# Doubles joined inside the next up product, shared tiles at every second place, and four products moved between the second batch's turned rows

## The chip, the cores and the metric

The kernel runs on one core of a Trainium2 chip. The metric is the device time of one execution in microseconds (us). Three executions of the kernel before gave 403.53, 402.61 and 404.11 us. One further execution was recorded by the profiler, and all rows below come from it.

## What is computed

The reference is a block of two parts over x of shape (4, 512, 512); cut to what matters:

```python
# part 1, once for each of the 4 batches
sim = einsum(h @ Wq.T, h @ Wk.T) / scale           # 512 x 512
thr = the 153rd largest value of each row of sim
A   = sigmoid(sim) * (sim >= thr);  A = (A + A.T) / 2
x   = x + tanh(g_xattn) * ((1 - gamma) * layernorm(x) + gamma * A)
# part 2, over all 2048 rows of x2 = layernorm(x)
shared = (silu(x2 @ Wsg) * (x2 @ Wsu)) @ Wsd
top_val, top_idx = top_k(x2 @ router_w, 2)         # 8 experts
each row, weighted by sigmoid(top_val), goes through 2 of the 8 experts:
    (silu(gate) * up) @ down_w[e]
x = x + tanh(g_ffn) * (shared + sum of the row's 2 experts)
```

## The kernel before, in words

Every engine runs a list of calls that is written out by hand. Semaphores tie the lists together; nothing reorders them.

Part 1 goes batch by batch: `sim_tile` products, copied out by ScalarE (`sim_of`); a search for the threshold on VectorE (`count`, `move`, `last_count`, `best_below`, `threshold`) with help from ScalarE (`sign`); `mask_sim`; `turn_a` (transposes) and `add_turned`; layer norm (`normal`); `turn_x2`; `route` (router logits), `turn_logits`, `pick_experts`, and the tables that tell which row goes to which expert (`rank_pairs`, `one_hots`, `table`, `add_table`, `count_pairs`, `order_columns`, `name_rows`, `read_plan`). The tables are finished twice: `read_plan(0)` after two batches names the rows of the first 9 expert tiles, `read_plan(1)` after all four those of the other 25.

Part 2 is a list of 50 jobs `j`, each of 128 rows. 16 of them are shared-expert tiles ("S"), 34 are expert tiles ("M", tile `t`). From j = 23 on (t = 7) there are only expert tiles and j = t + 16. One expert tile passes through these steps:

- GpSimd: `gather(t)`, an indirect DMA of 128 rows into one of 4 slots
- VectorE: `weight_of(t)`, the row's weight
- TensorE: `turn_rows(t)` (4 transposes), `up(j)` (gate and up products), `turn_h(j)`, `down(j)`
- ScalarE: `turned_rows`, `silu_of(j)`, `turned_h(j)`, and `y_of(j)`, which writes the result to one of two buffers `y_sb[:, j % 2]`
- VectorE: `gate(j)`
- GpSimd: `scatter(t)`, an indirect DMA that adds 128 rows to the output

Scatters add to shared rows, so each waits for the one before it to land (`pool.wait_ge(scattered, 16 * t)`), and `y_of(j)` waits until the scatter of job j - 2 has landed. In a row of the trace a scatter is `out_dram<-y_sb,idx` (or `y_sb,tmp`) on L550, and a shared tile's plain store is on L512. TensorE's steps on neighbouring jobs interleave: `up(j+1)`, `turn_rows`, `down(j)`, `turn_h(j+1)`.

Nine of the expert tiles are mixed: their 128 rows are four units of 32 rows, each with an expert of its own (the word "shared tiles" in the title means these). A mixed tile's products run as groups 32 columns wide (L1288 and L1318) instead of 128 wide (L1292 and L1327). Its weights are first copied side by side: `stage_up` on VectorE (4 copies of 128x2048, L2014) and `stage_down` on ScalarE (4 copies of 128x1024, L783). Both stages have one buffer, so copies for the next mixed tile start only after the product of the last one. A mixed tile may hold a token twice ("doubles"). `fold(j)` on TensorE adds doubles up (one product on `y_sb`, L1244), and `folded_y(j)` on ScalarE copies the sum back (L787); only then may its scatter start. Before, the mixed tiles are t = 9, 12, 15, 18, 21, 24, 27, 30, 32.

A shared tile's `gate(j)` writes `hT[:, j % 2]` and waits for the `down` of job j - 2 (`dve.wait_ge(y_ps, j - 1)`), which reads the same half.

Of the kernel before, what the change touches and what calls it, by code (L numbers as in the profile page):

```python
# [16 lines left out]
P = 128  # L17
# [8 lines left out]
def flamingo_gated_block(nc, x, ctx_in, g_xattn, g_ffn, wq, wk, gamma_raw, router_w, gate_up_w, down_w,  # L26
# [38 lines left out]
    MIXED = (9, 12, 15, 18, 21, 24, 27, 30, 32)  # L65
# [14 lines left out]
    NJ = len(JOBS)  # L80

# [9 lines left out]
    def x_slot(j):  # L91
        kind, n = JOBS[j]
        return n % RT if kind == "S" else 2 + n % 2

# [16 lines left out]
    with ExitStack() as stack:  # L111
# [123 lines left out]
        etab_u = tmp[0:1, 3, 64:64 + UNITS].bitcast(I32)  # L235
        unit_gu = sim[:, :, :, :].rearrange("p b i n -> p b (i n)")
# [232 lines left out]
        def _(pool):  # L469
# [38 lines left out]
            def shared(j):  # L508
# [3 lines left out]
                G.dma_start(out_v[n // RT][:, n % RT], y_sb[:, j % 2], accum_op=ALU.add).then_inc(shared_out[j % 2], 16)  # L512
# [21 lines left out]
            def scatter(t):  # L534
# [7 lines left out]
                if t == 0:  # L542
                    for m in range(2):
                        pool.wait_ge(shared_out[m], 16 * RT)
                else:
                    pool.wait_ge(scattered, 16 * t)
                if t == EARLY:
                    for m in range(2):
# [3 lines left out]
                                     in_=y_sb[:, j % 2, :], in_offset=None, compute_op=ALU.add  # L552
# [101 lines left out]
        def _(act):  # L654
# [110 lines left out]
            def y_of(j):  # L765
                act.wait_ge(y_ps, j + 1)
                if j >= 2:
                    if is_m(j - 2):
                        act.wait_ge(scattered, 16 * m_count(j - 1))
                    else:  # L770
                        act.wait_ge(shared_out[j % 2], 16 * s_count_like(j))
                A.activation(y_sb[:, j % 2], y_b[j % 2][:, :], ACT.Copy, scale=gates[:, 1:2]).then_inc(y_done, 1)  # L772
# [12 lines left out]
            def folded_y(j):  # L785
                act.wait_ge(fold_ps, mixed_at(j) + 1)
                A.copy(y_sb[:, j % 2], f_b[0][:, :]).then_inc(folded, 1)  # L787
# [62 lines left out]
            sign(2, 0)  # L850
            y_of(1)
# [8 lines left out]
            sim_of(3, 2)  # L860
# [3 lines left out]
            sign(2, 1)  # L864
            sign(2, 2)
            probs(1)
            sim_of(3, 3)
            silu_of(4)
            silu_of(5)
            sign(2, 3)  # L870
            silu_of(6)
            affine(2)
            y_of(3)
            y_of(4)
            read_bad(2)
            turned_rows(0)
            silu_of(7)
            turned_rows(1)
# [68 lines left out]
            turned_rows(7)  # L947
            silu_of(21)
            y_of(19)
            silu_of(22)  # L950
            turned_rows(8)
            silu_of(23)
            y_of(20)
# [20 lines left out]
            stage_down(1, 1)  # L974
            silu_of(27)
            turned_rows(12)
            folded_y(25)
# [7 lines left out]
            turned_h(28)  # L985
            silu_of(29)
# [1351 lines left out]
```

## Time and profile before

| what | value |
|---|---|
| median of three runs | 403.53 us (402.61 to 404.11) |
| the profiled execution's own time | 402.77 us |
| its span, first to last instruction | 401.0 us |
| TensorE busy | 367.5 us, 92% of the span |
| VectorE, ScalarE, GpSimd busy | 228.9, 216.8, 134.1 us |
| granted TensorE clock, mean | 0.975 |

The span is what the rows of the trace describe; 1.8 us of the execution's own time lie around it. "PE" is TensorE, "PEld" its weight loads, "DVE" VectorE, "ACT" ScalarE, "POOL" GpSimd, "SP" the queue that issues plain DMAs. A row of a timeline gives start, duration, engine, line, operation and tiles, and in brackets how long the engine was idle before it and what ended the idle time. In the chain of work, durations are cut so that the pieces follow one another.

### The profile page before, as it was taken

Reading aid. Unit: us, or ns where it says so; the run is one execution under the profiler, and the core shown is the slowest. Engines: PE = TensorE matmul, PEld = TensorE weight load, DVE = VectorE, ACT = ScalarE, POOL = GpSimd, SP = SyncE. Lnnn points to the kernel's source line nnn. Section 1 sums busy time; section 2 is a strip of 40 time slices with the busy share of each in tenths; the row PEclk is TensorE's granted clock in tenths of the full one; section 3 lists DMA queues with packets and bytes.
Section 4 is the critical chain, followed back from the end, with each engine's and each line's share of the span. In section 5 each row is a group of like instructions: output and inputs, shape, how many; then the busy total and the mean of one; then the engine's idle time right before and its main releaser. Section 6 shows DMA issues by size and latency. Waiting matters only on the chain.

```text
span 401.0 us, 6566 instructions
## 1 busy us (share of the span) xinstructions
PE 367.5 (92%) x2018; PEld 202.8 (51%) x2021; DVE 228.9 (57%) x819; ACT 216.8 (54%) x422; POOL 134.1 (33%) x114
## 2 busy tenths in 40 slices
PE   8859889889999999999999999999999999998950
PEld 4314478467755688548955444444444444433310
DVE  1899999998998689852636652332415150505000
ACT  3594877484773696353121475455555647363620
POOL 2201121110534331322303363544536354544231
PEclk9977999999999999999999999999999999999995
DMA  7999971084676542467423444535354454544432
GB/s 215 384 386 382 391 249 13 15 242 130 188 133 184 161 76 32 52 147 172 50 33 79 80 63 97 83 77 107 54 106 66 93 86 78 103 65 96 52 45 33
DMA packets 29353, 51.12 MB, mean 127 GB/s; under 512 B 4614, under 2 KB 7942, under 8 KB 29318
## 3 DMA queue, kind: packets, MB, share of 16 engines
q0 software_dynamic: 9920, 22.16, 32.9%
q1 hardware_dynamic: 19110, 28.40, 20.2%
q8 instruction: 17, 0.28, 0.3%
q14 instruction: 18, 0.15, 0.1%
q10 hardware_dynamic: 288, 0.13, 0.1%
HBM read 28.60 MB, written 22.09 MB: 126 GB/s over the span
## 4 chain that ended last, share of the span: by engine, by line
PE 74%; DMA 9%; DVE 7%; ACT 4%; issue 3%; SPq 1%; POOLq 0%; POOL 0%; DVEq 0%; ACTq 0%
PE gate_up L1292 20%; PE down L1327 15%; PE gate_up L1281 14%; PE gate_up L1288 6%; DMA out_dram<-y_sb,idx 4%; PE turned_x L1263 4%; DMA out_dram<-y_sb,tmp 4%; PE down L1318 3%; PE turned_h L1302 2%; DMA xs<-in_x_dram 2%; PE down L1117 2%; DVE ge_words L1721 2%; PE front L1244 1%; PE front L1155 1%; ACT x L711 1%
## 5 line engine op out<-in xcount | busy, mean ns | idle before, releaser
L1292 PE MATMUL gate_up<-w_gu,xT 128*128 x200 | 89.9, 593 | 0.8 <-DVE hT L2036 0.7
L550 POOL DMA_INDIRECT out_dram<-y_sb,idx x25 | 49.6, 1985 | 73.9 <-DMA out_dram<-y_sb,tmp 26.6
L2031 DVE SCALAR_TENSOR_TENSOR h<-gate_up,p_t,silu 128x256 f32<-128x256 f32 x34 | 16.4, 482 | 80.9 <-ACT silu L745 72.0
L1281 PE MATMUL gate_up<-xT,w_shgu 128*128 128x128 f32 x512 | 59.9, 276 | 1.1 <-ACT xT L722 1.1
L1281 PEld LDWEIGHTS gate_up<-xT,w_shgu 128*128 128x128 f32 x512 | 58.6, 192 | 3.3 <-issue 2.0
L772 ACT ACTIVATE y_sb<-down,gates 128x512 f32<-128x512 f32 x50 | 34.2, 687 | 43.4 <-PE down L1327 28.4
L1292 PEld LDWEIGHTS gate_up<-w_gu,xT 128*128 128x128 f32 x200 | 36.3, 190 | 39.2 <-issue 39.1
L529 POOL DMA_INDIRECT xg<-x_rows,idx x34 | 40.2, 1182 | 36.4 <-DMA x_rows<-payl 15.5
L1327 PE MATMUL down<-w_dn,hT 128*128 x100 | 47.2, 596 | 0.0
L745 ACT ACTIVATE silu<-gate_up,p_t 128x256 f32<-128x256 f32 x34 | 16.1, 473 | 49.1 <-PE gate_up L1292 31.7
L2014 DVE COPY sim<-w_gu 128x2048 f32 x36 | 41.9, 1223 | 0.3 <-issue 0.2
L674 ACT ACTIVATE junk<-sim,probe 128x512 int8<-128x512 f32 x44 | 31.2, 713 | 13.3 <-DVE probe L1712 9.7
L783 ACT COPY xs<-w_dn 128x1024 f32 x36 | 36.0, 1045 | 0.5 <-issue 0.3
L1288 PE MATMUL gate_up<-sim,xT 128*32 128x512 f32 x288 | 32.8, 595 | 0.0
L763 ACT COPY xT<-turned_x 128x512 f32<-128x512 f32 x34 | 19.9, 585 | 20.0 <-PE turned_x L1263 19.3
L1327 PE MATMUL down<-w_shdn,hT 128*128 128x512 f32 x64 | 30.3, 599 | 0.0
L512 POOL DMA_DIRECT2D out_dram<-y_sb x16 | 15.7, 1025 | 42.4 <-ACT y_sb L772 42.3
L1263 PEld LDWEIGHTS turned_x<-ident,xg 128*128 128x128 f32 x136 | 16.0, 141 | 20.2 <-issue 19.9
L550 POOL DMA_INDIRECT out_dram<-y_sb,tmp x9 | 14.2, 1576 | 34.4 <-DVE p_junk L2021 26.3
L1327 PEld LDWEIGHTS down<-w_dn,hT 128*128 128x128 f32 x100 | 17.2, 190 | 13.3 <-issue 13.3
L2021 DVE SCALAR_TENSOR_TENSOR p_junk<-xg,oh_e 128x8 f32<-128x8 f32 x34 | 5.4, 161 | 30.1 <-DMA xg<-x_rows,idx 29.9
L1263 PE MATMUL turned_x<-ident,xg 128*128 128x128 f32 x136 | 21.0, 277 | 1.2 <-ACT xT L763 0.8
(222 smaller groups left out, 508.3 us busy)
## 6 DMA issues: line engine op xcount, KB each, us to landing
w_gu<-in_L_ffn_gate_up_w_dram SPq DMA_DIRECT2D x8, 1024.0 KB, 12.2
xs<-in_x_dram SPq DMA_DIRECT2D x4, 1024.0 KB, 6.4
w_dn<-in_L_ffn_down_w_dram SPq DMA_DIRECT2D x8, 512.0 KB, 10.7
out_dram<-xs SPq DMA_DIRECT2D x4, 1024.0 KB, 6.4
x_rows<-x SPq DMA_DIRECT2D x4, 1024.0 KB, 5.1
out_dram<-y_sb POOLq DMA_DIRECT2D x16, 256.0 KB, 4.4
w_gu<-in_ctx_dram SPq DMA_DIRECT2D x4, 256.0 KB, 5.3
xg<-x_rows,idx POOLq DMA_INDIRECT x34, 4.1
```

The lines of the kernel that those rows point to most:

```text
L529: G.indirect_dma_start(out=xg[:, t % XG, :], out_offset=None, in_=x2_rows[0:2 * N, :] if t < EARLY else x2_rows[:, :], in_offset=bass.Indi ...
L550: G.indirect_dma_start(out=out[0:2 * N, :] if t < EARLY else out[:, :], out_offset=bass.IndirectOffsetOnAxis(ap=rows, axis=0), in_=y_sb[:, ...
L674: ins = A.activation(junk[:, i - SHARE[b]], sim[:, b, i], ACT.Sign, scale=-1.0, bias=probe[:, k, i:i + 1], accum_out=sgn[:, k, i:i + 1])
L763: A.copy(xT[:, x_slot(j)], x_b[:, :].rearrange("p (c t) -> p c t", c=DC)).then_inc(xt_done, 1)
L772: A.activation(y_sb[:, j % 2], y_b[j % 2][:, :], ACT.Copy, scale=gates[:, 1:2]).then_inc(y_done, 1)
L783: A.copy(unit_dn[:, g], w_dn[:, bass.ds(e * (IC * D), IC * D)]).then_inc(dn_staged, 1)
L1263: mm = TE.transpose(x_b[:, c * P:(c + 1) * P], xg[:, t % XG, c * P:(c + 1) * P], ident[:, :])
L1281: mm = TE.matmul(g_b[j % 2][:, f * P:(f + 1) * P], w_shgu[:, c, f * P:(f + 1) * P], xT[:, x_slot(j), c], start=(c == 0), stop=(c == DC - 1))
L1288: mm = TE.matmul(g_b[j % 2][at, :], xT[:, x_slot(j), c, at], unit_gu[:, r, c * F2:(c + 1) * F2], start=(c == 0), stop=(c == DC - 1))
L1292: mm = TE.matmul(g_b[j % 2][:, :], xT[:, x_slot(j), c], w_gu[:, bass.ds(experts[n] * (DC * F2) + c * F2, F2)], start=(c == 0), stop=(c == ...
L1327: mm = TE.matmul(y_b[j % 2][:, :], hT[:, j % 2, c], w, start=(c == 0), stop=(c == IC - 1))
L2014: V.tensor_copy(unit_gu[:, g], w_gu[:, bass.ds(e * (DC * F2), DC * F2)]).then_inc(gu_staged, 1)
```

## The change

Four things are changed; the amount of arithmetic is not.

1. The mixed tiles move to t = 9, 11, 13, ..., 25. The last eight tiles (26 to 33) are then all ordinary ones. `stage_up`, `stage_down`, `folded_y` and `fold` move with them.
2. `fold(j)` is no longer a call of its own between `up` and `turn_rows`. It is issued in the middle of `up(j + 2)`, and `folded_y(j)` stands ahead of `silu_of(j + 2)`.
3. Around the second batch (`route(1)`, `turn_logits(1)`, `table(0)`) and in the plan of the later tiles (`order_columns(1)`, `order_units`, `name_rows(1)`) calls change places on TensorE, VectorE and ScalarE; `warm(4, 3)`, three products that compute nothing, is gone.
4. `CHAIN`, `Y_FROM`, `y_slot`, `y_user` and `y_at` are new names. `CHAIN` lists 0 to 33 in order and `Y_FROM` is 100 while jobs end at 49, so every wait and every address comes out as before.

```diff
-    MIXED = (9, 12, 15, 18, 21, 24, 27, 30, 32)
+    MIXED = (9, 11, 13, 15, 17, 19, 21, 23, 25)
...
-            def up(j):
+            def up(j, folds=None):
...
                     for c in range(DC):
+                        if c == DC // 2 and folds is not None:
+                            fold(folds)
...
             turn_a(1, 3)
+            pe.wait_ge(sim_ready, 14)
+            sim_tile(3, 2)
             down(1)
-            pe.wait_ge(sim_ready, 14)
+            pe.wait_ge(sim_ready, 15)
             rank_pairs(0)
             down(2)
+            pe.wait_ge(rank_used, 1)
+            sim_tile(3, 3)
...
-            pe.wait_ge(rank_used, 1)
-            sim_tile(3, 2)
+            down(3)
             route(1)
-            pe.wait_ge(y_done, 2)
-            warm(4, 3)
             turn_logits(1)
+            table(0)
             up(4)
...
             up(21)
             pe.wait_ge(logit_used, 4)
             count_pairs(1)
+            down(19)
+            order_columns(1)
             up(22)
-            order_columns(1)
             pe.wait_ge(rank_used, 4)
             table(3)
-            down(19)
             turn_rows(7)
+            down(20)
             order_units()
             turn_rows(8)
             up(23)
             name_rows(1)
-            down(20)
             up(24)
...
-            up(27)
-            fold(25)
+            up(27, 25)
             turn_rows(12)
...
             last_count(2)
-            gate(6)
+            gate(7)
             best_below(2)
             weight_of(0)
-            gate(7)
             threshold(2)
...
             place_units()
+            gate(22)
             read_plan(1)
-            gate(22)
...
             gate(31)
-            stage_up(3, 0)
-            stage_up(3, 1)
-            stage_up(3, 2)
-            stage_up(3, 3)
+            stage_up(4, 0)
+            stage_up(4, 1)
+            stage_up(4, 2)
+            stage_up(4, 3)
             weight_of(17)
```

What stands there in the order of instructions, at three places.

TensorE while the plan of the later tiles is made, before; `down1` is `down(19)`, `gate_up0` is `up(22)`, L1203 is `order_columns(1)`, L1194 `table(3)`, L1207 `order_units`, and the two L1263 are `turn_rows(7)` and `turn_rows(8)`:

```order
L1281 MATMUL gate_up0<-xT,w_shgu 128x128 x16
L1203 MATMUL front1<-el_b,upper 128x1
L1194 MATMUL front0<-tmp 128x128 x8
L1327 MATMUL down1<-w_shdn,hT 128x512 x2
L1254 TENSOR_LOAD etab
L1254 ISA x2
L1263 MATMUL turned_x<-ident,xg 128x128 x4
L1207 MATMUL front1<-el_b,upper 128x1
L1254 TENSOR_LOAD etab
L1254 ISA x2
L1263 MATMUL turned_x<-ident,xg 128x128 x4
```

The same place after the change:

```order
L1349 MATMUL down1<-w_shdn,hT 128x512 x2
L1221 MATMUL front1<-el_b,upper 128x1
L1299 MATMUL gate_up0<-xT,w_shgu 128x128 x16
L1212 MATMUL front0<-tmp 128x128 x8
L1272 TENSOR_LOAD etab
L1272 ISA x2
L1281 MATMUL turned_x<-ident,xg 128x128 x4
L1349 MATMUL down0<-w_shdn,hT 128x512 x2
L1225 MATMUL front1<-el_b,upper 128x1
L1272 TENSOR_LOAD etab
L1272 ISA x2
L1281 MATMUL turned_x<-ident,xg 128x128 x4
```

`down(19)` went ahead of `up(22)` and `order_columns(1)` with it; `down(20)` (`down0`), which stood behind `name_rows(1)`, now stands between the two turned rows.

TensorE at the first fold, before: the last half of the ordinary product `up(27)`, the fold (L1244), then `turn_rows(12)` and `down(26)`:

```order
L1292 ISA
L1292 MATMUL gate_up1<-w_gu,xT 128x512
L1292 ISA
L1292 MATMUL gate_up1<-w_gu,xT 128x512
L1244 MATMUL front0<-y_sb,x2 128x512
L1263 MATMUL turned_x<-ident,xg 128x128 x4
L1327 ISA
L1327 MATMUL down0<-w_dn,hT 128x512
L1327 ISA
L1327 MATMUL down0<-w_dn,hT 128x512
```

After the change, `down(25)`, `turn_h(26)`, and then `up(27)`, which is now a mixed tile:

```order
L1340 MATMUL down1<-xs,hT 32x512 x8
L1324 MATMUL turned_h<-ident,h 128x128 x2
L1308 MATMUL gate_up1<-sim,xT 32x512 x8
L1262 MATMUL front0<-y_sb,x2 128x512
L1308 MATMUL gate_up1<-sim,xT 32x512 x8
L1272 TENSOR_LOAD etab
L1272 ISA x2
L1281 MATMUL turned_x<-ident,xg 128x128 x4
```

The fold, 128 wide, now stands between the two halves of a product in groups 32 wide. This is so for 8 of the 9 folds; the ninth stands inside the ordinary `up(43)`.

VectorE around the end of the third batch's search, before; `hT<-gate_up0` is `gate(6)`, `hT<-gate_up1` is `gate(7)`, the rows with `tmp<-ge_words` and `top8<-tmp` are `best_below(2)`:

```order
L1745 SCALAR_TENSOR_TENSOR bad<-cnt,u 128x4
L2036 TENSOR_TENSOR hT<-gate_up0,silu 128x256
L1758 SCALAR_TENSOR_TENSOR tmp<-ge_words,sim 128x512 x2
L1762 MAX top8<-tmp 128x8 x2
L1758 SCALAR_TENSOR_TENSOR tmp<-ge_words,sim 128x512 x2
L1762 MAX top8<-tmp 128x8 x2
L2021 SCALAR_TENSOR_TENSOR p_junk,p_t<-xg,oh_e 128x8
L2036 TENSOR_TENSOR hT<-gate_up1,silu 128x256
L1767 SCALAR_TENSOR_TENSOR sel8,thr<-iota,u,top8 128x8 x4
```

After the change:

```order
L1756 SCALAR_TENSOR_TENSOR bad<-cnt,u 128x4
L2047 TENSOR_TENSOR hT<-gate_up1,silu 128x256
L1769 SCALAR_TENSOR_TENSOR tmp<-ge_words,sim 128x512 x2
L1773 MAX top8<-tmp 128x8 x2
L1769 SCALAR_TENSOR_TENSOR tmp<-ge_words,sim 128x512 x2
L1773 MAX top8<-tmp 128x8 x2
L2032 SCALAR_TENSOR_TENSOR p_junk,p_t<-xg,oh_e 128x8
L1778 SCALAR_TENSOR_TENSOR sel8,thr<-iota,u,top8 128x8 x4
```

`gate(7)` went ahead of `best_below(2)`, and `gate(6)` ahead of `last_count(2)`.

## Rows read from the trace of the kernel before

**Rows 1.** The page: span, the chain that ended last, the costliest groups.

```profile
span 401.0 us, 6566 instructions
...
PE 74%; DMA 9%; DVE 7%; ACT 4%; issue 3%; SPq 1%; POOLq 0%; POOL 0%; DVEq 0%; ACTq 0%
...
L772 ACT ACTIVATE y_sb<-down,gates 128x512 f32<-128x512 f32 x50 | 34.2, 687 | 43.4 <-PE down L1327 28.4
```

**Rows 2.** Busy time by stretch: length, PE, PEld, DVE, ACT, POOL, clock, DMA.

```profile
80.00:110.00 30.00, 27.81 (x224) 22.20 (x226) 27.53 (x138) 20.85 (x47) 7.41 (x8) 1.00 0.63 187
...
197.43:213.17 15.74, 14.16 (x115) 9.49 (x113) 5.52 (x29) 2.34 (x6) 3.02 (x3) 1.00 0.26 34
...
319.54:338.40 18.86, 18.86 (x95) 8.04 (x95) 6.52 (x13) 10.35 (x18) 9.68 (x7) 1.00 0.47 85
...
355.00:401.00 46.00, 30.23 (x158) 11.57 (x156) 7.11 (x15) 17.16 (x28) 14.83 (x9) 0.89 0.36 56
```

**Rows 3.** Timelines of VectorE and TensorE in the third batch.

```profile
108.22 0.42 DVE L2036 TENSOR_TENSOR hT<-gate_up,silu 128x256 f32<-128x256 f32 x1 [0.57 <-PE down L1327]
...
118.47 2.73 DVE L1802 SCALAR_TENSOR_TENSOR xs<-sim,c,xs 128x512 f32<-128x512 f32 x4
121.22 1.41 DVE L1812 SCALAR_TENSOR_TENSOR xs<-front,c,xs 128x512 f32<-128x512 f32 x2
...
123.10 1.04 PE L1155 MATMUL front<-ident,sim 128*128 128x128 f32 x8
```

**Rows 4.** Timeline of TensorE, plan of the later tiles.

```profile
204.70 0.63 PE L1263 MATMUL turned_x<-ident,xg 128*128 128x128 f32 x4 [0.76 <-ACT xT L763]
...
213.17 3.69 PE L1292 MATMUL gate_up<-w_gu,xT 128*128 x8 [0.70 <-DVE hT L2036]
```

**Rows 5.** The chain of work, 319 to 336 us: start, duration, what.

```profile
319.60 3.57 PE gate_up L1288 x32
323.17 0.59 PE turned_x L1263 x4
323.75 1.72 PE down L1327 x4
325.47 0.22 PE turned_h L1302 x2
325.69 3.44 PE gate_up L1292 x8
329.13 0.44 PE turned_x L1263 x4
329.56 1.85 PE down L1318 x16
331.42 0.37 PE turned_h L1302 x2
...
335.22 0.86 PE front L1244 x2
```

**Rows 6.** Timeline of TensorE, the last 32 us.

```profile
370.79 1.12 PE L1244 MATMUL front<-y_sb,x 128*128 128x512 f32 x2 [1.29 <-ACT y_sb L772]
...
383.24 0.44 PE L1302 MATMUL turned_h<-ident,h 128*128 128x128 f32 x2
```

**Rows 7.** Timeline of GpSimd, the last 58 us: scatters.

```profile
343.87 2.82 POOL L550 DMA_INDIRECT out_dram<-y_sb,idx  x1 [2.58 <-DMA out_dram<-y_sb,tmp]
...
350.50 1.58 POOL L550 DMA_INDIRECT out_dram<-y_sb,idx  x1 [1.88 <-DMA out_dram<-y_sb,idx]
...
363.27 3.43 POOL L550 DMA_INDIRECT out_dram<-y_sb,idx  x1 [2.65 <-DMA out_dram<-y_sb,tmp]
...
370.74 1.58 POOL L550 DMA_INDIRECT out_dram<-y_sb,idx  x1 [2.72 <-ACT y_sb L772]
...
392.72 1.55 POOL L550 DMA_INDIRECT out_dram<-y_sb,idx  x1 [3.66 <-DMA out_dram<-y_sb,tmp]
```

**Rows 8.** Timeline of VectorE, the last copies.

```profile
361.97 4.64 DVE L2014 COPY sim<-w_gu 128x2048 f32 x4
```

More of the change, by code:

```diff
@@ L80, in flamingo_gated_block @@
     NJ = len(JOBS)
+    Y_FROM = 100
+    assert Y_FROM % 2 == 0
     def mixed_at(j):
@@ L93, in x_slot, with y_slot, y_user @@
         return n % RT if kind == "S" else 2 + n % 2
+    def y_slot(j):
+        return j % 2 if j < Y_FROM else (j - Y_FROM) % 3
+    def y_user(j):
+        last = [k for k in range(j) if y_slot(k) == y_slot(j)]
+        return last[-1] if last else None
     def job_of(kind, n):
@@ L766, in y_of @@
                 act.wait_ge(y_ps, j + 1)
[L767 to L772, printed above, removed]
+                k = y_user(j)
+                if k is not None and is_m(k):
+                    act.wait_ge(scattered, 16 * CHAIN.index(JOBS[k][1]) + 16)
+                elif k is not None:
+                    act.wait_ge(shared_out[k % 2], 16 * s_count_like(k) + 16)
+                if y_slot(j) == 2 and k is None:
+                    act.wait_ge(scatter_ready, 1)
+                A.activation(y_at(j), y_b[j % 2][:, :], ACT.Copy, scale=gates[:, 1:2]).then_inc(y_done, 1)
             def stage_down(m, g):
@@ L985, in _ @@
             turned_h(28)
+            stage_down(2, 0)
+            stage_down(2, 1)
+            folded_y(27)
             silu_of(29)
@@ L1002, in _ @@
             turned_h(31)
+            stage_down(3, 2)
+            stage_down(3, 3)
             silu_of(32)
@@ L1019, in _ @@
             turned_h(34)
+            stage_down(5, 0)
+            stage_down(5, 1)
+            folded_y(33)
             silu_of(35)
@@ L1053, in _ @@
             turned_h(40)
+            stage_down(8, 0)
+            stage_down(8, 1)
+            folded_y(39)
             silu_of(41)
@@ L1291, in up @@
                     for c in range(DC):
+                        if c == DC // 2 and folds is not None:
+                            fold(folds)
                         mm = TE.matmul(g_b[j % 2][:, :], xT[:, x_slot(j), c],
@@ L1643, in _ @@
             turn_h(47)
-            fold(46)
             up(48)
@@ L2110, in _ @@
             normal_in(2)
+            gate(3)
             weigh_experts(0)
@@ L2246, in _ @@
             stage_up(2, 3)
+            weight_of(13)
+            gate(28)
             weight_of(14)
             gate(29)
+            stage_up(3, 0)
+            stage_up(3, 1)
+            stage_up(3, 2)
+            stage_up(3, 3)
             weight_of(15)
```

189 lines of the change are left out of this document (82 added, 107 removed).

## The prediction

> **What bounds the kernel now.** I read the page first. The span is 401.0 us, and TensorE makes 74% of the chain that ended last [rows 1]. Then I read busy time by stretch. Between 319.54 and 338.40 us, TensorE is busy for all 18.86 us; the same length and business come back in five stretches of three tiles each, from 244 to 338 us. So there only TensorE's own work counts. Three other places differ: 80 to 110 us, where TensorE is busy 27.81 of 30.00 us and VectorE 27.53; 197.43 to 213.17 us, with 14.16 of 15.74; and the last 46 us, with only 30.23 [rows 2].
>
> The last 46 us are read on GpSimd's timeline. From scatter(29) at 370.74 to scatter(33) at 392.72 us the four steps take 21.98 us, 5.5 us each, and each scatter was released by the landing of the one before [rows 7]. So the end is a chain of scatters. TensorE had even waited 1.29 us for it at 370.79 us, in the fold of tile 30 [rows 6]. The span ends 401.0 - 392.72 = 8.3 us after the last scatter starts.
>
> **The change, term by term**, on the profiled execution's scale: span 401.0 us, time 402.77 us, so 1.8 us around the span. Its time is 0.76 us below the median of the three runs.
>
> *Second batch, 80 to 110 us: 0 us.* TensorE idles 2.19 us here [rows 2], and the change fills idle time with `sim_tile(3, 2)`, `sim_tile(3, 3)` and `down(3)`. By my walk through the calls TensorE is about 1.4 us earlier at `up(8)`. But VectorE has only 2.5 us of idle time in these 30 us, and it must deliver the third batch. `best_below(2)` began after `gate(6)` at 108.22 us. After the change `gate(7)` stands there. It waits for `down(5)`, which stands behind `turn_rows(0)`, and my walk puts it at 109.0, so `best_below(2)` starts about 0.8 us later than before. All behind it on VectorE moves along: `gate(7)` itself (0.4 us) is then already done, but ScalarE's values wait for the search too. `add_own(2)` started at 118.47 and took 2.73 us, and the first half of the pair at 121.22 released `turn_a(2, 2)`, which TensorE began at 123.10 us [rows 3]. With 0.8 us more the release comes at 118.5 + 0.8 + 2.7 + 0.7 + 0.2 = 122.9 us. So TensorE cannot be more than 0.2 us ahead there. What was won is waited away at transposes. Bounds: if best_below is not later, all 1.4 us stay; if it is later than I think, up to 1 us is lost.
>
> *Plan of the later tiles: -1.5 us.* The instructions are the same and TensorE idled 15.74 - 14.16 = 1.58 us [rows 2]: 0.76 us at `turn_rows(8)`, where ScalarE had not copied the rows turned just before, and 0.70 us at `up(24)`, which waited for `gate(22)` [rows 4]. `down(20)` between the two turned rows covers the first wait. The second goes because `gate(22)` now needs a `down(20)` that is done 5 us earlier; its place ahead of `read_plan(1)` costs nothing, since `name_rows(1)` is still running on TensorE. What is late next is the first gather of the second plan: it starts as `stage_up(0, 0)` does, and `turn_rows(9)` wants its rows 2 us earlier. So of the 1.58 us I take 1.5, with bounds 0 (the gather holds `turn_rows(9)` by as much) and 2.2 (short gaps below the profile's waits close too).
>
> *Mixed tiles at every second place: 0 us on TensorE.* Eight mixed tiles lie behind `up(27)` before and after, the same work in another order. Two covers get thinner, with these rows. `stage_up` takes 4.64 us [rows 8] and must fit between one mixed `up` and the next: 0.59 + 1.72 + 0.22 + 3.44 + 0.44 + 1.85 + 0.37 = 8.6 us [rows 5], and with about 1 us for silu and gate ahead of it, 3 us are left. `gate` of the ordinary tile stands behind the copies and is wanted when its `up` and silu are done, 6.5 us after the mixed `up`: 5.7 us are used, 0.8 us are left. `stage_down` ends some 3.2 us after `down` of the tile before (0.69 us of `y_of` [rows 1], about 0.4 of `turned_h`, two copies of about 1 us, estimates for the starts between them), and the mixed `down` starts 0.22 + 3.44 + 0.44 = 4.1 us after it: 0.9 us are left. If a cover is gone, its lack is paid 8 times. ScalarE is busy 10.35 us in 18.86 [rows 2], and about 9 in 13.3 after.
>
> *Folds inside `up`: +2.2 us, and +0.9 us for one more fold ahead of the last `down`s.* The fold is 0.86 us wherever it stands [rows 5]. But the chain shows a price for going between 128-wide and 32-wide groups. Into a mixed product: 3.57 against 3.44 us, 1.85 against 1.72, so 0.13 us. Out of it: transposes 0.59 against 0.44, `turn_h` 0.37 against 0.22, so 0.15 us [rows 5]. Before, the fold stood among wide products and paid nothing; now 8 of 9 folds stand inside a narrow one and pay both ways, 8 x 0.28 = 2.2 us. The bounds are 0 (if the price belongs to something else at these borders, such as the first weights) and twice this, 4.5 us. The ninth fold came behind `down(48)` before, and all nine now come ahead of it: 0.86 us.
>
> The Trainium skill, page "TensorEngine Tiling (Array Packing)", section "Key Properties", says that a change of tiling mode, not just of tile, drains TensorE. By that rule each fold inside a mixed product drains it twice; it gives no duration. It speaks against this edit, and the sum by the rows alone is the one above; without the rule and the border price the sum would be 2.2 us lower.
>
> *The end.* `down(48)` ended at 383.24 us [rows 6]. Now: 383.24 - 1.5 (plan) + 2.2 (borders) + 0.9 (ninth fold) - 1.3 (no wait at the fold of tile 30) = 383.5 us. TensorE arrives no earlier. But the scatters do. The last eight tiles are ordinary, 3.44 + 0.44 + 1.72 + 0.22 = 5.8 us apart, more than a step of 5.5 us, and no fold of 1.9 us or more stands between `y_of` and a scatter. So scatter(31) comes straight behind `y_of(47)`: `down(47)` ends 0.22 + 3.44 + 1.72 = 5.4 us ahead of `down(48)`, at 378.1; 0.69 us of `y_of` [rows 1] and some 0.5 us for starts give 379.3 us. It was 392.72 - 2 x 5.5 = 381.7 us. Then two steps of 5.5 and the 8.3 us behind the last scatter: 379.3 + 11.0 + 8.3 = 398.6 us. That is 2.4 us below 401.0, so 400.4 us on this execution's scale and 401.1 us on the median's; I say 401.0. `CHAIN` and `Y_FROM` change no wait: 0.
>
> **Rivals.**
>
> *The borders are free* (20%). The fold is one product into a bank of its own, and its neighbours' weights may be loaded ahead. For it: only four kinds of border are seen, none with a wide product inside one narrow product. Against: all four agree within 0.02 us. Sum: 401.1 - 2.2 = 398.9 us.
>
> *The second batch's gain stays* (15%), because VectorE also loses its 0.57 us wait at 108.22 us [rows 3]: 401.1 - 1.4 = 399.7 us. Both of these together (7%): 397.5 us.
>
> *The plan gains nothing* (10%): the gather is late. 401.1 + 1.5 = 402.6 us.
>
> *The chain of scatters takes over between tiles 9 and 25* (8%), the one that ends slower. A scatter issued while `stage_up` copies takes longer to issue: 2.82 us and a step of 6.63 us at 343.87, 3.43 us and 7.47 us at 363.27, 1.3 us into the copies at 361.97, against 1.58 and 5.5 us elsewhere [rows 7, 8]. Copies now come in every pair of tiles. TensorE needs 18.86 - 5.82 + 0.28 = 13.3 us a pair. One slow scatter gives 5.5 + 6.6 = 12.1 us, hidden. Two slow ones give 14.1 us: 0.8 us late in each of 8 pairs, 6.4 us, of which the last tiles make up 6 x 0.3 = 1.9, so 401.1 + 4.5 = 405.6 us. It decides once a pair of steps passes 13.3 us by more than 0.5 us. Against it: by my walk the mixed tile's scatter starts 4.2 us into its pair and is issued at 5.8, as the copies begin at 5.7 us, and the ordinary one starts at 9.8, half a microsecond ahead of their end.
>
> The Trainium skill, page "SBUF — State Buffer", section "Who interferes with whom", says that such a VectorE copy and GpSimd hold a shared port pair by turns, whoever starts first for a whole instruction. By that rule a scatter that starts just ahead of the copies is not held, as I have the mixed one; one that slips 1 us is.
>
> **How the numbers follow.** The likeliest case has 40% and a range of its own of 400.0 to 402.3 us. With the two faster rivals and their sum at the low end and the late gather at the high end, 397.2 to 403.8 us leaves out some 2 in 10. Half a per cent, 2.0 us, is about what a measurement can tell from no change: below 401.5 us lie the three faster cases and more than half of the likeliest (64%), above 405.5 only the scatter chain (8%), the rest is 28%.
>
> **What would show it.** A pair of tiles, mixed `up` to mixed `up`, takes 13.3 us if the borders cost, 13.05 if not; in the chain of work the two halves of a mixed `up` and its fold add up to 4.7 us, not 4.4. TensorE shows no wait between 197 and 213 us and begins `up(27)` at 235.8 us, not 237.34. At `turn_a(2, 2)` it stands at 122.9 to 123.2 us with a wait for VectorE. From scatter(26) on no scatter takes more than 1.6 us to issue, and scatter(31) starts at about 379.3 us. I would be wrong if TensorE waits for `silu`, `gate` or the staged weights in each pair (a cover of 0.8 or 0.9 us gone), if the second batch holds more than 0.5 us, or if the last scatters are not 5.5 us apart.

## The result, and the profile after

The changed kernel takes 400.13 us (median of 6 runs, 398.39 to 400.76), the kernel before 403.54 us (median of 6, 402.61 to 404.11). The ratio is 0.9913, with a 95% interval of 0.9890 to 0.9936: 3.5 us or 0.9% less. 401.0 was predicted, with a range of 397.2 to 403.8. The time came out near the forecast, but three terms of the sum did not: their errors partly cancelled, which is luck, as shown below.

The page of the changed kernel: its span, and the shares of the chain that ended last. They answer to [rows 1].

```profile
span 397.9 us, 6563 instructions
PE 65%; DMA 11%; DVE 9%; ACT 8%; issue 4%; SPq 1%; POOLq 0%; POOL 0%; DVEq 0%; ACTq 0%
```

TensorE's share of the chain fell from 74% to 65%, and transfers rose from 9% to 11%: more of the end hangs on something other than products. Busy time by stretch has the columns of [rows 2].

```profile
80.00:110.00 30.00, 28.01 (x227) 22.22 (x227) 28.23 (x139) 20.21 (x46) 8.98 (x9) 1.00 0.70 198
200.00:225.00 25.00, 25.00 (x171) 14.48 (x171) 13.67 (x52) 7.37 (x14) 7.97 (x7) 1.00 0.44 66
319.54:332.90 13.36, 13.36 (x75) 5.01 (x74) 5.75 (x11) 8.43 (x14) 6.62 (x5) 1.00 0.45 80
355.00:397.90 42.90, 28.80 (x86) 13.48 (x84) 2.67 (x11) 9.99 (x20) 12.99 (x9) 0.91 0.38 57
```

TensorE idles 1.99 us in the second batch's stretch, and not at all from 200 to 225 us or in a pair of tiles (319.54 to 332.90 us). In the last 43 us it is busy only 28.80.

*Second batch.* TensorE's timeline at `turn_a(2, 2)`, then VectorE's rows that release it. The row at 121.77 us is the one that stood at 123.10 in [rows 3].

```profile
120.06 1.88 PE L1349 MATMUL down<-w_shdn,hT 128*128 128x512 f32 x4
121.77 1.04 PE L1173 MATMUL front<-ident,sim 128*128 128x128 f32 x8
...
107.92 0.42 DVE L2047 TENSOR_TENSOR hT<-gate_up,silu 128x256 f32<-128x256 f32 x1
108.27 1.28 DVE L1769 SCALAR_TENSOR_TENSOR tmp<-ge_words,sim 128x512 f32<-128x512 uint8 x2
...
117.94 2.73 DVE L1813 SCALAR_TENSOR_TENSOR xs<-sim,c,xs 128x512 f32<-128x512 f32 x4
120.58 1.41 DVE L1823 SCALAR_TENSOR_TENSOR xs<-front,c,xs 128x512 f32<-128x512 f32 x2
```

There is no bracket with idle time, so `turn_a(2, 2)` follows `down` at once. VectorE's first half was done at 120.58 + 0.71 = 121.3 us.

*Plan of the later tiles.* TensorE's timeline, to be read against [rows 4]; the last row is `down(20)` in the kernel before.

```profile
202.49 1.88 PE L1349 MATMUL down<-w_shdn,hT 128*128 128x512 f32 x4
...
204.24 0.63 PE L1281 MATMUL turned_x<-ident,xg 128*128 128x128 f32 x4
...
209.65 3.70 PE L1314 MATMUL gate_up<-w_gu,xT 128*128 x8
...
210.48 1.98 PE L1327 MATMUL down<-w_shdn,hT 128*128 128x512 f32 x4
```

`turn_rows(8)` at 204.24 waits for nothing; it waited 0.76 us before. `up(24)` starts at 209.65 instead of 213.17 us. The row at 202.49 is `down(20)` at its new place.

*A pair of tiles*, mixed `up` to mixed `up`, on TensorE's timeline.

```profile
260.36 1.92 PE L1308 MATMUL gate_up<-sim,xT 128*32 128x512 f32 x16
262.22 1.12 PE L1262 MATMUL front<-y_sb,x 128*128 128x512 f32 x2
263.27 1.92 PE L1308 MATMUL gate_up<-sim,xT 128*32 128x512 f32 x16
265.13 0.66 PE L1281 MATMUL turned_x<-ident,xg 128*128 128x128 f32 x4
...
273.75 1.50 PE L1308 MATMUL gate_up<-sim,xT 128*32 128x512 f32 x12
```

It takes 273.75 - 260.36 = 13.39 us, and the two halves with their fold 265.13 - 260.36 = 4.77 us.

*The end.* GpSimd's timeline: scatters 24, 25, 26, 31 and 33 (to be read against [rows 7]).

```profile
337.24 1.58 POOL L566 DMA_INDIRECT out_dram<-y_sb,idx  x1 [2.70 <-DMA out_dram<-y_sb,tmp]
344.70 1.58 POOL L566 DMA_INDIRECT out_dram<-y_sb,tmp  x1 [4.56 <-ACT y_sb L805]
350.05 1.58 POOL L566 DMA_INDIRECT out_dram<-y_sb,idx  x1 [2.45 <-DMA out_dram<-y_sb,tmp]
...
378.55 1.55 POOL L566 DMA_INDIRECT out_dram<-y_sb,idx  x1 [4.01 <-DMA out_dram<-y_sb,idx]
...
389.50 1.55 POOL L566 DMA_INDIRECT out_dram<-y_sb,idx  x1 [3.91 <-DMA out_dram<-y_sb,idx]
```

And the same in the chain of work: start, length, what.

```profile
340.73 1.72 PE gate_up L1314 x4
342.45 0.87 PE front L1262 x2
343.35 0.59 ACT y_sb L805
343.97 0.52 issue
344.70 4.58 DMA out_dram<-y_sb,tmp
349.32 0.73 issue
350.05 4.83 DMA out_dram<-y_sb,idx
```

The chain leaves TensorE at the last fold, the one inside `up(43)` (L1262), goes through its copy `folded_y(41)` (L805) to scatter(25) at 344.70 us, and from there runs as landing, issue, landing to the end: (389.50 - 344.70) / 8 = 5.60 us a step. `y_of(47)` on ScalarE is what I had expected scatter(31) to follow:

```profile
376.27 0.69 ACT L790 ACTIVATE y_sb<-down,gates 128x512 f32<-128x512 f32 x1 [1.13 <-PE down L1349]
```

It ended at 376.96, and scatter(31) came 1.6 us later, released by the landing of the scatter ahead.

### The profile page after: what moved, and what is told of

The parts are those of the page before. It is cut to its first block, busy times and chain, and to the rows that moved or that the text cites. A ratio compares the mean times of both kernels' runs of the same rounds, so it can differ in the third digit from the quotient of the medians.

```text
span 397.9 us, 6563 instructions
## 1 busy us (share of the span) xinstructions
PE 368.6 (93%) x2018; PEld 200.8 (50%) x2018; DVE 228.0 (57%) x819; ACT 216.8 (54%) x422; POOL 132.8 (33%) x114
## 4 chain that ended last, share of the span: by engine, by line
PE 65%; DMA 11%; DVE 9%; ACT 8%; issue 4%; SPq 1%; POOLq 0%; POOL 0%; DVEq 0%; ACTq 0%
PE gate_up L1314 14%; PE down L1349 13%; PE gate_up L1299 12%; DMA out_dram<-y_sb,idx 8%; PE gate_up L1308 8%; PE down L1340 4%; PE turned_x L1281 3%; ACT junk L690 3%; PE front L1262 2%; PE turned_h L1324 2%; DMA xs<-in_x_dram 2%; PE front L1173 1%; ACT x L727 1%; DMA out_dram<-y_sb,tmp 1%; ACT sim L685 1%
## 5 line engine op out<-in xcount | busy, mean ns | idle before, releaser
L566 POOL DMA_INDIRECT out_dram<-y_sb,idx x25 | 42.4, 1697 | 71.5 <-DMA out_dram<-y_sb,idx 33.6
L545 POOL DMA_INDIRECT xg<-x_rows,idx x34 | 45.2, 1329 | 43.5 <-DMA x_rows<-payl 13.5
L1308 PE MATMUL gate_up<-sim,xT 128*32 128x512 f32 x288 | 34.4, 598 | 0.0
L566 POOL DMA_INDIRECT out_dram<-y_sb,tmp x9 | 15.2, 1687 | 37.9 <-ACT y_sb L805 35.1
L1324 PEld LDWEIGHTS turned_h<-ident,h 128*128 128x128 f32 x68 | 8.6, 141 | 18.3 <-issue 17.0
```

The costliest lines, as they stand in the source:

```text
L545: G.indirect_dma_start(out=xg[:, t % XG, :], out_offset=None, in_=x2_rows[0:2 * N, :] if t < EARLY else x2_rows[:, :], in_offset=bass.Indi ...
L566: G.indirect_dma_start(out=out[0:2 * N, :] if t < EARLY else out[:, :], out_offset=bass.IndirectOffsetOnAxis(ap=rows, axis=0), in_=y_at(j) ...
L1308: mm = TE.matmul(g_b[j % 2][at, :], xT[:, x_slot(j), c, at], unit_gu[:, r, c * F2:(c + 1) * F2], start=(c == 0), stop=(c == DC - 1))
```

## The experiments

Each kernel was timed beside the kernel before on the same chip. Ratios are to it. A trace holds one execution, and its opening is not steady: VectorE's first row of batch statistics, which waits for the input, starts between 9.81 and 11.55 us over the thirteen traces. So places are compared from one point of TensorE's work to the next. The kernel before was timed again in each group of runs, with medians of 403.5 to 404.2 us, and two kernels of different groups are compared only through their ratios. Ratios are turned into us with 403.5. In the table all are us: "search" is from that first row of VectorE to the start of `turn_a(2, 2)`, "plan" from there to `up(24)`, "later" on to `up(27)`, "tiles" on to the start of scatter(33).

| kernel | ratio, 95% interval | first row | search | plan | later | tiles |
|---|---|---|---|---|---|---|
| before | 1 | 10.39 | 112.71 | 90.07 | 24.17 | 155.38 |
| changed | 0.9913 (0.9890 to 0.9936) | 10.45 | 111.32 | 87.88 | 23.95 | 155.90 |
| e1_second | 0.9974 (0.9957 to 0.9991) | 11.09 | 111.29 | 90.10 | 24.16 | 155.48 |
| e2_plan | 0.9956 (0.9938 to 0.9974) | 10.58 | 113.22 | 87.83 | 23.85 | 155.52 |
| e3_tiles | 1.0029 (1.0011 to 1.0048) | 10.62 | 112.45 | 90.03 | 24.25 | 156.04 |
| e4_fold_after | 0.9905 (0.9879 to 0.9931) | 9.96 | 111.34 | 87.88 | 23.95 | 155.08 |
| e5_gate7 | 0.9911 (0.9877 to 0.9945) | 10.21 | 111.82 | 87.84 | 23.94 | 156.57 |
| e6_short_up | 0.9907 (0.9881 to 0.9932) | 11.40 | 111.80 | 87.84 | 23.95 | 156.21 |
| e7_no_ninth | 0.9854 (0.9827 to 0.9881) | 9.93 | 111.83 | 87.85 | 23.95 | 154.57 |
| e8_no_tiles | 0.9875 (0.9850 to 0.9900) | 11.55 | 111.40 | 87.87 | 23.85 | 155.60 |
| e9_fold_quarter | 0.9899 (0.9877 to 0.9921) | 10.94 | 111.33 | 87.88 | 23.95 | 155.03 |
| e10_old_tiles_fold_in | 0.9858 (0.9834 to 0.9883) | 9.81 | 111.92 | 87.85 | 23.86 | 153.82 |
| e11_old_tiles_quarter | 0.9852 (0.9828 to 0.9876) | 10.97 | 111.34 | 87.91 | 23.86 | 153.86 |

From scatter(33) to the end of the span it is 8.3 us before and 8.4 in the changed kernel.

### The three parts one at a time

**e1_second**: before, with the edits around the second batch alone.

```diff
             turn_a(1, 3)
+            pe.wait_ge(sim_ready, 14)
+            sim_tile(3, 2)
             down(1)
...
+            down(3)
             route(1)
-            warm(4, 3)
             turn_logits(1)
+            table(0)
             up(4)
...
             last_count(2)
-            gate(6)
+            gate(7)
             best_below(2)
```

> The kernel before with the second batch's part of the change alone (the products, the mapped tiles and the gates of 76 to 110 us). The recorded step said that what is won there is waited away at turn_a(2, 2): time as before, 0 us, and TensorE at that transpose no earlier than 122.9 us. The theory formed from the trace of after is that it stays, since best_below(2) starts 0.3 us earlier and not 0.8 later: 1.3 us faster than before, a ratio of 0.997, turn_a(2, 2) at about 121.8 us.

Measured: 0.9974, or 1.0 us less (0.4 to 1.7). "Search" is 111.3 us against 112.7. The gain is made and stays.

**e2_plan**: before, with the edits to the plan of the later tiles alone.

```diff
+            down(19)
+            order_columns(1)
             up(22)
...
             turn_rows(7)
+            down(20)
             order_units()
...
+            gate(22)
             read_plan(1)
```

> The kernel before with the part around order_columns(1), order_units and name_rows(1) alone. The recorded step said -1.5 us with bounds 0 and -2.2; the trace of after (up(24) at 209.65 instead of 213.17 us, of which 1.3 us came from the second batch) says -2.2 us, a ratio of 0.9945. The rival that the first gather is late gives 0 us.

Measured: 0.9956, or 1.8 us less (1.0 to 2.5). "Plan" is 87.83 us against 90.07, and "later" 0.3 us shorter.

**e3_tiles**: before, with the mixed tiles at every second place and the folds inside `up` alone.

```diff
-    MIXED = (9, 12, 15, 18, 21, 24, 27, 30, 32)
+    MIXED = (9, 11, 13, 15, 17, 19, 21, 23, 25)
...
-            up(27)
-            fold(25)
+            up(27, 25)
```

> The kernel before with the mixed tiles at every second place and the folds inside up alone. The recorded sum gives it -2.4 + 1.5 = -0.9 us. If second batch and plan give 1.3 and 2.2 us, the whole change's 3.4 us leave nothing for it: 0 us, a ratio of 1.000. A rival is that it loses, since each fold inside a mixed up pays two borders: +1 us or more.

Measured: 1.0029, or 1.2 us more (0.4 to 1.9); "tiles" is 0.7 us longer. This part, the one that the change is named after, costs time.

**e8_no_tiles**: the changed kernel with the mixed tiles and the folds as before, so the first two parts together.

```diff
-    MIXED = (9, 11, 13, 15, 17, 19, 21, 23, 25)
+    MIXED = (9, 12, 15, 18, 21, 24, 27, 30, 32)
...
-            up(27, 25)
+            up(27)
+            fold(25)
```

> The kernel before with the second batch's part and the plan's part, but with the mixed tiles and folds where they were. By the positions of TensorE in the traces (turn_a(2, 2) 1.3 us earlier, from there to up(27) 2.4 us shorter, from up(27) to the end 163.7 us in the kernel before and 164.3 in the changed one) it should be 3.7 us faster than before, a ratio of 0.991, and 0.6 us faster than the changed kernel. If the tiles' part brings 0.9 us as the recorded sum had it, this kernel is 0.9 us slower than the changed one, 0.993 or more.

Measured: 0.9875, against 0.9913 of the changed kernel: 0.0038 x 403.5 = 1.5 us less without the third part. The two intervals meet at 0.989 to 0.990, but e3_tiles, whose interval leaves out 1, says the same from the other side. That the third part costs time is shown; its size is known less well. In the traces "tiles" is 155.4 to 155.6 us in the four kernels with the old order and the old folds, and 155.9 to 156.6 in the three with the new ones and nothing else changed there (changed, e3_tiles, e5_gate7): 0.7 us on average. Nor do the ratios of the parts add up: e1_second and e2_plan give 1.0 + 1.8 = 2.8 us, and e8_no_tiles, which has both, 0.0125 x 403.5 = 5.0 us (4.0 to 6.1), where its trace is 1.3 + 2.5 = 3.8 us shorter up to `up(27)`. Where the rest comes from is open.

The losses of the old order are still there: GpSimd's scatters 27 to 29, and the copies of `stage_up` on VectorE.

```profile
355.04 1.60 POOL L550 DMA_INDIRECT out_dram<-y_sb,tmp  x1 [4.05 <-DVE p_junk L2019]
360.72 3.30 POOL L550 DMA_INDIRECT out_dram<-y_sb,idx  x1 [2.76 <-DMA out_dram<-y_sb,tmp]
368.07 1.58 POOL L550 DMA_INDIRECT out_dram<-y_sb,idx  x1 [2.73 <-ACT y_sb L772]
...
359.29 4.64 DVE L2012 COPY sim<-w_gu 128x2048 f32 x4
```

Scatter(28) starts 1.4 us into four copies, takes 3.30 us instead of 1.58 to issue, and the step to scatter(29) is 7.35 us.

### The second batch: does the place of gate(7) matter?

**e5_gate7**: the changed kernel, with `gate(7)` back behind `best_below(2)`.

```diff
-            gate(7)
             best_below(2)
             weight_of(0)
+            gate(7)
```

> The changed kernel with gate(7) back behind best_below(2). The recorded step rests on gate(7) delaying best_below(2). In the changed kernel best_below(2) began at 108.27 us right behind gate(7), and TensorE did not wait at turn_a(2, 2). If gate(7) costs VectorE only its own 0.34 us, best_below(2) starts 0.3 us earlier, TensorE stands where it did, and the time stays within 0.5 us of the changed kernel's. If VectorE's place decides what of the second batch's gain is kept, the kernel is 0.5 us or more away from it.

Measured: 0.9911, as the changed kernel. Counted from VectorE's first row, `best_below(2)` began 0.4 us earlier (107.67 - 10.21 = 97.46 against 108.27 - 10.45 = 97.82 us), yet "search" is 111.8 us, not less than 111.3. The other kernels with this part have 111.3 to 111.9 us as well, so "search" alone says nothing here. A shorter stretch does. From the start of `down(5)` to `turn_a(2, 2)` the nine other kernels with this part take 15.83 to 15.85 us, and this one 122.03 - 105.87 = 16.16 us. TensorE's timeline shows why: `up(9)`, at 113.09 us, waited 1.03 us for `gate(7)`. In the changed kernel it waits for nothing, and TensorE waits 0.78 us for ScalarE's turned rows instead, a little later. So the place of `gate(7)` is worth 0.3 us, too little to be seen in the time, and it counts by TensorE's wait for it, not by VectorE's search.

### What a fold inside a mixed product costs

**e4_fold_after**: the changed kernel, with eight folds behind the mixed `up` (next to the transposes, which are 128 wide anyway) and `folded_y` behind `turned_rows`.

```diff
-            up(27, 25)
+            up(27)
+            fold(25)
             turn_rows(12)
...
-            folded_y(25)
             silu_of(27)
             turned_rows(12)
+            folded_y(25)
```

> The changed kernel with eight folds issued behind their mixed up and folded_y behind turned_rows, as before the change; the ninth stays inside up(43). If a fold between two halves of a mixed product pays 0.28 us for two borders, a pair of tiles takes 13.1 instead of 13.39 us and the kernel is 8 x 0.28 = 2.2 us faster than the changed one, a ratio to before of 0.986. If the price belongs to something else at the borders, the pair stays at 13.4 us and the time at that of the changed kernel, 0.991. A third way: the later scatter of a mixed tile slows the chain of scatters, and the kernel is slower than the changed one by 1 us or more.

TensorE's timeline of one pair in this kernel:

```profile
246.22 3.64 PE L1308 MATMUL gate_up<-sim,xT 128*32 128x512 f32 x32
249.79 1.12 PE L1262 MATMUL front<-y_sb,x 128*128 128x512 f32 x2
250.76 0.60 PE L1281 MATMUL turned_x<-ident,xg 128*128 128x128 f32 x4
...
259.32 1.92 PE L1308 MATMUL gate_up<-sim,xT 128*32 128x512 f32 x16
```

The pair takes 259.32 - 246.22 = 13.10 us against 13.39. So a fold inside a product of 32-wide groups costs 0.29 us more than one beside 128-wide work, in one direction and back; 0.28 was predicted. But the time is 0.9905 against 0.9913, no difference that can be told, and "tiles" is 0.8 us shorter where 8 x 0.29 = 2.3 us of TensorE's work is gone. The scatters say why. One of a mixed tile, with VectorE's copies at that time:

```profile
266.33 2.65 POOL L566 DMA_INDIRECT out_dram<-y_sb,tmp  x1 [3.41 <-ACT y_sb L805]
...
264.02 4.63 DVE L2033 COPY sim<-w_gu 128x2048 f32 x4
```

Seven scatters now start 2.3 us into the copies and take 2.5 to 2.65 us, and at the end the chain of scatters sets the time: scatter(25) is released by the landing of scatter(24) and starts only 1.2 us earlier, counted from `up(27)`, and the eight steps behind it last 45.14 us instead of 44.80.

### What sets the end

**e6_short_up**: the changed kernel, with half of the contraction of `up` left out in the last four jobs: 4 x 1.7 = 6.9 us less work for TensorE.

```diff
-                    for c in range(DC):
+                    chunks = range(DC) if j < 46 else (0, DC - 1)
+                    for c in chunks:
```

> The changed kernel with the up products of the last four jobs (46 to 49) cut to two of their four parts, 1.7 us less TensorE work in each; it leaves out half of the contraction there. If the end is the chain of scatters that began at scatter(25), as the trace of after shows (each released by the landing before it from scatter(26) on), the time stays that of the changed kernel, within 0.3 us, with scatter(31) at 378.5 us as before. If the last y_of decide, as the recorded sum has it (scatter(31) straight behind y_of(47)), scatter(31) starts some 3 us earlier and the kernel is 1.3 us or more faster.

Measured: 0.9907, as the changed kernel. The last `down` on TensorE:

```profile
380.53 1.98 PE L1350 MATMUL down<-w_dn,hT 128*128 x4 [3.38 <-ACT hT L770]
```

Counted from `up(27)`, it starts 3.6 us earlier (145.54 against 149.13 us), having waited 3.38 us, and the last scatter is not earlier (156.21 against 155.90). TensorE does not bound the end of the changed kernel; that is shown.

**e7_no_ninth**: the changed kernel without the ninth fold and its copy; the doubles of tile 25 aren't joined, which leaves that sum out.

```diff
-            up(43, 41)
+            up(43)
...
-            folded_y(41)
```

> The changed kernel without the ninth fold and its copy; it leaves out the joining of doubles in the tile t = 25. If the late scatter(25) (344.70 us, behind its fold) is what sets the end, scatter(25) starts right after scatter(24) lands, about 342.8 us, scatter(26) at 348 us, and from there y_of sets the pace: 1.3 us faster in the span, of which 0.86 us are also saved on TensorE. If the fold of the last mixed tile does not matter, the time stays the same within 0.3 us.

```profile
342.80 1.58 POOL L566 DMA_INDIRECT out_dram<-y_sb,tmp  x1 [2.71 <-DMA out_dram<-y_sb,idx]
348.36 1.58 POOL L566 DMA_INDIRECT out_dram<-y_sb,idx  x1 [2.66 <-DMA out_dram<-y_sb,tmp]
```

These are scatters 25 and 26. Scatter(25) is now released by the scatter ahead, and counted from `up(27)` it starts 1.9 us earlier than in the changed kernel, the last one 1.3 us. The median fell by more, to 0.9854, which is 0.0059 x 403.5 = 2.4 us; the trace of one execution shows about half of it.

**e9_fold_quarter**: the changed kernel, with every fold one quarter of a product earlier.

```diff
-                        if c == DC // 2 and folds is not None:
+                        if c == 1 and folds is not None:
```

> The changed kernel with every fold behind the first quarter of its up product instead of behind its half. The borders of the folds are still paid, so TensorE's work is the same. Theory (the end is a chain of scatters that begins with the scatter of tile 25, which is held by the last fold; without that fold it issued at 342.80 us instead of 344.70): the last fold comes 0.93 us earlier (a quarter of an up product of 3.7 us), the scatter of tile 25 issues at about 343.8, the last one at about 388.6, and the kernel takes 0.9 us less than the changed one: a ratio to the kernel before of about 0.989. Rival (TensorE's work sets the end): the last down product ends at 381.4 as before, and the ratio stays at 0.991.

Measured: 0.9899; with these intervals that can't be told from 0.9913. In the trace scatter(25) and scatter(33) both come 0.87 us earlier after `up(27)`, as the theory asked. For scatter(25) that is clear: in the four kernels with its fold in the middle it starts at 111.10 us. For scatter(33) it is near the 0.7 us by which two executions with the same end differ. The chain has almost caught up with TensorE:

```profile
372.38 1.55 POOL L566 DMA_INDIRECT out_dram<-y_sb,idx  x1 [3.87 <-ACT y_sb L790]
```

Scatters 30 to 32 are each released by `y_of` of their own tile. So TensorE would be the next limit, and moving the last fold still earlier could bring little more; that was not run.

### A version that is faster than both

**e10_old_tiles_fold_in**: e8_no_tiles, with seven folds in the middle of the next *ordinary* `up`, where their neighbours are as wide as they are, and `folded_y` ahead of `silu_of`.

```diff
-            up(27)
-            fold(25)
+            up(27, 25)
...
+            folded_y(25)
             silu_of(27)
             turned_rows(12)
-            folded_y(25)
```

> The kernel of e8_no_tiles (second batch and plan changed, mixed tiles at their old places) with its seven folds moved from behind the product into the middle of the next ordinary up product, which has 128-wide groups like the fold, so that no border between widths is added. Theory (the end is the chain of scatters, and the wait of 1.28 us for the fold at 368.13 and the slow issue of the scatter of tile 28, 3.30 us beside four copies of VectorE, are in it): the scatter of tile 27 is released by the one ahead at about 353.6 instead of 355.04 (1.4 us), that of tile 28 is issued ahead of the copies at 1.6 instead of 3.3 us (1.7 us): up to 3 us less than e8_no_tiles, a ratio of about 0.980. Rival (TensorE's work bounds the end, the waits of the chain only fill its slack): the last down product ends where it did, the ratio stays within 0.002 of 0.9875.

**e11_old_tiles_quarter**: the same, with `c == 1` in place of `c == DC // 2`.

> The kernel of e10_old_tiles_fold_in with the folds behind the first quarter of the up product. Theory of the scatter chain: if a fold is still the last thing that its scatter waits for, 0.9 us less than e10_old_tiles_fold_in; if the scatter ahead already releases it, as I expect, the same time within 0.3 us. Rival (the earlier fold meets VectorE's copies of the product that it joins and waits for them on TensorE): up to 0.5 us more.

Measured: 0.9858 and 0.9852, medians 398.25 and 397.98 us; the second is 0.6% below the changed kernel (0.9913), and the intervals do not meet. Against e8_no_tiles "tiles" is 1.8 us shorter in both; the ratios differ by 0.7 and 0.9 us, which the intervals don't tell from zero. Up to 3 us were expected. e10's chain of work shows where the rest stayed:

```profile
363.39 1.90 PE down L1320 x16
365.31 0.70 ACT y_sb L772
366.05 1.14 PE front L1244 x2
367.21 0.59 ACT y_sb L787
367.84 0.72 issue
368.56 4.91 DMA out_dram<-y_sb,tmp
373.52 0.50 issue
374.23 4.40 DMA out_dram<-y_sb,idx
378.63 0.70 ACT y_sb L772
379.37 1.14 PE front L1244 x2
380.54 0.59 ACT y_sb L787
381.16 0.71 issue
```

Scatter(29) comes 4.45 us earlier than in e8_no_tiles, counted from `up(27)`, but scatter(32) only 1.9. Between them the chain meets TensorE again: tiles 30 and 32 are mixed, and each of their scatters waits for `down`, `y_of`, fold and copy in a row (381.16 - 378.63 = 2.5 us for the last three). At 378.63 the chain comes from the landing of scatter(31), but `y_of(48)` waits only for scatter(30), which had landed at 368.56 + 4.91 = 373.5 us. What held it is `down(48)`, which ended at 378.50 us, 0.13 us ahead, the same distance as from `down(46)` (365.18) to `y_of(46)` (365.31). Both theories held a part: the scatters had slack to give back, and TensorE bounds what is left. A quarter or a half makes no difference, as expected.

## Why the prediction came out as it did

The changes of the span from before, in five pieces: to `turn_a(2, 2)` -1.3, to `up(24)` -2.2, to `up(27)` -0.2, from there to scatter(33) +0.5 and behind it +0.1; in all -3.1 us. The prediction had 0, -1.5 for plan and later together, and -0.9 for the rest, -2.4 in all. Two gains were taken too small, one loss was called a gain, and they partly cancelled.

*Second batch, 0 us: wrong, and the step is "So TensorE cannot be more than 0.2 us ahead there".* The ten traces with this part have 111.3 to 111.9 us (mean 111.5), the three without 112.5 to 113.2 (mean 112.8): 1.3 us are kept. In e2_plan, the one with 113.2 us, the granted clock was 0.94 from 80 to 110 us and 1.00 in the others; without it the gain is 1.0 us. `best_below(2)` started at 108.27 us, not 0.8 us later but 0.3 us earlier than before (108.56); my walk put `gate(7)` at 109.0 and it ran at 107.92. `add_own(2)` was 0.5 us earlier than in [rows 3], and VectorE's first half was done at 121.3 us, 121.5 with the 0.2 us that my sum adds, instead of 122.9. e5_gate7 shows that I had looked for the harm of `gate(7)` on the wrong engine: ahead of the search it costs VectorE 0.4 us that TensorE does not feel, and behind the search TensorE waits for it and loses 0.3 us. There was a hint in [rows 3]: `turn_a(2, 2)` had no idle time ahead of it before the change, so it was TensorE, not VectorE, that it waited for. VectorE's release, 121.22 + 0.7 + 0.2 = 122.1 us, left 1.0 us, and the 0.8 us that I added took it away. This was the rival with 15%.

*Plan, -1.5 us: the mechanism right, the size too small.* Both waits of [rows 4] are gone, TensorE is busy 25.00 of 25.00 us, and the gain to `up(27)` is 2.4 us. e2_plan alone shows the same 2.2 and 0.3. The term that was sized wrong is the price of a wait: I took the idle time that the profile prints, 0.76 + 0.70 us. From the start of `down(20)` to what stands behind it TensorE took 213.17 - 210.48 = 2.69 us before and at most 204.24 - 202.49 = 1.75 us after, 0.94 us less for a printed wait of 0.70; and from `turn_rows(8)` to `up(23)` it is 205.44 - 204.70 = 0.74 us before and 204.71 - 204.24 = 0.47 after, on top of the printed 0.76. The idle time is printed only from the modelled end of the row before (1.98 us long), while without a wait the next row starts 1.75 us behind its start, so a wait costs more than is printed. My upper bound of 2.2 was right, but not for its reason: from `turn_a(2, 2)` to `up(24)` the time in which TensorE was not busy fell only from 1.99 to 0.42 us. The gather cost nothing. The rival "the plan gains nothing" is out. With it `up(27)` began at 233.60 and not at 235.8 us.

*Mixed tiles at every second place, 0 us on TensorE: right.* No wait for `silu`, `gate` or a stage appears in the pairs; the covers of 0.8 and 0.9 us held.

*Folds inside `up`, +2.2 and +0.9 us: right on TensorE.* The pair takes 13.39 us (13.3 predicted, 13.05 if borders were free), the halves with the fold 4.77 (4.7), and e4_fold_after gives 0.29 us a fold by taking the borders away. That is shown for TensorE; the time did not fall by 8 times as much. The Trainium skill's "TensorEngine Tiling (Array Packing)", "Key Properties", which has a change of mode drain TensorE, agrees with this; the number is only in the traces. With the measured gains in place of mine, my sum for the end of `down(48)` becomes 383.5 - 1.3 - 0.9 = 381.3 us, and it ended at 381.4. So TensorE's part of the sum was sound.

*The end: wrong, and the step is "So scatter(31) comes straight behind `y_of(47)`".* It started at 378.55 us, which is close to my 379.3, but for another reason. `y_of(47)` was done at 376.96, and 0.5 us later the scatter would have been due; the chain of scatters was still 1.1 us late. Two things were missed. I looked at the last tiles only, where no fold stands, and not at where the chain enters them: scatter(25) waits until 344.70 us for the last fold, a half product and a copy after its own `y_of`. And tiles 5.8 us apart leave the chain little to catch up with: from scatter(26) to scatter(31) its steps were (378.55 - 350.05) / 5 = 5.70 us, not 5.5, so it made up only 0.1 us a tile. e6_short_up shows that the end is not TensorE's. That the last fold sets it is shown by e7_no_ninth in the time and by e9_fold_quarter in the trace alone. So what the mixed tiles won by ending early was less than what the borders and the ninth fold cost. How much of the loss is the borders' is not shown: e4_fold_after took away 2.3 us of TensorE's work and won 0.8 us in the trace and nothing clear in the time. The prediction had this part at -0.9 us; it is +1.2 (0.4 to 1.9) by e3_tiles, +1.5 by e8_no_tiles and +0.7 by the traces.

*Why is the loss not the 3.1 us of borders and ninth fold?* A part of the answer is that the old order has losses of its own there, which e8_no_tiles shows; what each is worth was not measured: 1.28 us of TensorE waiting in a fold, as in [rows 6], and a scatter of 3.30 us. In the changed kernel, as predicted, no scatter from 26 on takes more than 1.6 us to issue.

*The rival that ended slower*, the chain of scatters taking over between tiles 9 and 25, did not come: the mixed scatters take 1.58 us from tile 11 on (tile 9's, at 238.28, takes 2.52) and the ordinary ones are a little slowed (1.86 us at 270.50). That it was not far is seen in e4_fold_after, where the mixed scatters start 2.3 us behind the start of the copies and not 1.5 us ahead of it, and take up to 2.65 us; there the chain has taken over from scatter(23) on. The Trainium skill's "SBUF — State Buffer", "Who interferes with whom", says that of such a copy and a GpSimd instruction the one that starts first has the shared ports for its whole length and the other is blocked. The rows agree: a scatter that started 1.3 us or more ahead of the copies took 1.58 us, and one that started among them ended at a fixed distance behind the end of a copy, wherever it had begun (see the last section).

## What to carry to other kernels

Before you cost a move of work away from the end, follow the serial chain of transfers back to the place where it last waited for an engine, and price that place: the last few steps run as late as they were entered. And when you price a wait, take the time between the instructions around it, not only the idle time printed. If a small product must stand inside another, choose a host of the same width; here the same fold cost 0.29 us more among 32-wide groups than beside 128-wide ones. And an instruction without idle time ahead of it tells that its other input was early: its row says which engine a gain in front of it will reach.

## What was new about the hardware

- A 128x512 product in two halves between groups 32 wide cost 0.29 us more than beside 128-wide work (pairs of 13.39 and 13.10 us).
- The issue of a 128-row scatter on GpSimd took 1.58 us alone. Beside four VectorE copies of 1.2 us, 4.64 us in all, it was the end of the issue that was fixed, not its length. Begun 0.7 to 1.1 us into the copies it ended 3.59 us behind their start, 0.1 us behind the third copy (2.82 us at 343.87 [rows 7], with copies from 343.10). Begun 1.2 to 1.4 us into them it ended at 4.73, 0.1 us behind the fourth (3.43 us in [rows 7, 8], 3.30 us in e8_no_tiles). Begun 2.3 us into them (e4_fold_after) it ended at 4.80 or 4.95. Begun in the last 0.4 to 0.9 us it ended 1.45 us behind the last copy (1.86 us at 270.50 in the changed kernel, with copies from 266.27 to 270.91). So a start 0.14 us later can end a whole copy later (1.09 us in, end at 3.59, in e1_second; 1.23 us in, end at 4.73, in e2_plan).
- A wait cost TensorE more than the idle time printed: 0.94 us for 0.70 behind `down(20)`. The row lasts 1.98 us when TensorE waits behind it, and without a wait the next row starts 1.75 us behind its start.
- In a chain of adding scatters of 128 rows a step took 5.60 us on average over eight in the changed kernel, 5.68 in e5_gate7 whose end is the same: 0.7 us of difference in the end of two executions from this alone.
- The start of VectorE's first statistics on the input moved between 9.81 and 11.55 us from one execution to another, so two spans 1 us apart can't be compared without it.
